# Grouped attention: own buffer for the query squares, result copies ahead of the upper halves, first lower half ahead of the next inverse sum

## The chip, the core and the metric

The kernel runs on one core of a Trainium2 chip. The metric is the time of one execution in microseconds (us) on the device; a shorter time is better. A core has five engines that run their own instruction streams and wait for each other through semaphores: TensorE (PE, matrix products, with PEld for its weight loads), VectorE (DVE), ScalarE (ACT), GpSimd (POOL) and SyncE (SP), which issues most DMAs.

## What is computed

The reference is a two layer block. Only the third stage is touched by the change, cross attention with grouped keys. Cut to that stage:

```python
q = (hidden_states @ Wq).reshape(B, S, N_HEADS, HEAD_DIM)            # B 4, S 256, 16 heads of 128
k = (encoder_hidden_states @ Wk).reshape(B, S_enc, N_KV_HEADS, HEAD_DIM)   # 1601 keys, 4 key heads
v = (encoder_hidden_states @ Wv).reshape(B, S_enc, N_KV_HEADS, HEAD_DIM)
q = rms_norm(q, q_norm_w)
k = rms_norm(k, k_norm_w)
scores = jnp.einsum('bqhd,bkhd->bhqk', q, jnp.repeat(k, 4, axis=2)) * scale
probs = jax.nn.softmax(scores, axis=-1)
out = jnp.einsum('bhqk,bkhd->bqhd', probs, jnp.repeat(v, 4, axis=2))
return out.reshape(B, S, N_HEADS * HEAD_DIM) @ Wo
```

Around it stand another attention, a mixture of experts and a quantized feed forward layer.

## The kernel before

`grouped_attention` works in 16 groups (4 batch rows times 4 key heads) of 8 steps, 128 steps in all, numbered n; s = n % 8 is the step within a group g. A step is one query head and one tile of 128 queries against all 1601 keys. A pair of steps (both query tiles of a head) is a unit u. Every value that goes into a product is split into an upper (HI) and a lower (LO) half, and each product is three matmuls.

The order on each engine is written out by hand; nothing is scheduled automatically. In step n:

- PE: `score(n)` fills the four banks of `ps_s`, and may start when ACT's first exponential of step n-1 has read them; then `weigh`, half of the value products of unit n//2 - 2, into `ps_m` (even n starts a unit and waits for `u_here`, odd n ends it); then the jobs of `plan[n]`, which prepare the next group in a ring of three banks `ps_t`: `kv` (keys and values), `q`, `qT` and `kT` (transposes), `y` (output product).
- DVE: `largest(n)` (maximum of the scores, `neg_max`); then its part of `plan[n-1]` (`entry`: copies, lower halves, sums of squares); `invert(n)`, the inverse of the row sum, which waits for both exponentials of step n; `probs_low(n-1)`, the lower halves of the probabilities of the step before in two pieces of 1024 and 577 columns.
- ACT: `exp(n, 0)`, `exp(n, 1)`; `probs_high(n)`, the upper halves, which wait for the inverse sum (`inverted`) and for the transposes of step n-2 (`turned_through`); `take_values` (odd n: `ps_m` to `out_n`, which raises `u_here`) or `split_result` (even n: `out_n` to `oT`, after which POOL subtracts); its part of `plan[n]` (`ring`); splits of weights (`split_q`, `split_kv`, `split_out`, each followed by a subtraction on POOL) in some steps.
- SP: per step one transposing DMA of the lower half of step n-1, then one of the upper half of step n, from `halves` to `pT`; and loads.

ACT's `ring` squares queries and keys into one buffer, `squares_of`, of two key places; a query job fills both. DVE sums them (`tensor_reduce` into `q_sq` or `k_sq`) and raises `squares`. The lines that guard the buffer:

```python
nth = nth_squared[e]
both = kind == "q" or (nth and squared[nth - 1][0] == "q")
if nth - (not both) > 0:
    act.wait_ge(squares, nth - (not both))
```

In a full group, step 0 prepares `qT`, `q`, `kv`; step 1 `q`, `kv` and `q_eps`; steps 2 and 3 two `kv` each (step 2 and 4 also `k_eps`, after which POOL scales); step 4 `kv`, `qT`; step 5 two `kT`; step 6 `y` and two `kT`; step 7 `y`. The last group has no `q`, `kv` or `kT` left to prepare.

Of the kernel before, what the change touches and what calls it, by code (L numbers as in the profile page):

```python
# [14 lines left out]
P = 128  # L15
# [1439 lines left out]
def grouped_attention(nc, side, mix, x_sb, eye, half_power, encoder_t, wq, wk, wv, wo, q_norm_w, k_norm_w):  # L1455
# [110 lines left out]

    squared = [e for n in range(-1, N + DRAIN) for e in plan[n] if e[0] in ("q", "kv")]
    nth_squared = {e: n for n, e in enumerate(squared)}

    with ExitStack() as ctx:  # L1570
        r = Room(nc, ctx, "ga")
# [26 lines left out]
        probs = [sb(f"probs{i}", [P, KV]) for i in range(PB)]  # L1598
        warm = sb("warm", [P, 1])
        squares_of = sb("squares_of", [P, 2, 2, DH])  # L1600
        part_max = sb("part_max", [P, 2])
        neg_max = sb("neg_max", [P, 2])
        half_sum = sb("half_sum", [P, 4, 2])
# [266 lines left out]
        def _(act):  # L1870
# [22 lines left out]
            def ring(e):  # L1893
                kind, m, g = e
                if kind in ("q", "kv"):
                    nth = nth_squared[e]
                    both = kind == "q" or (nth and squared[nth - 1][0] == "q")
                    if nth - (not both) > 0:

                        act.wait_ge(squares, nth - (not both))  # L1900
                act.wait_ge(*filled(e))
                if kind == "q":
                    nc.scalar.activation(squares_of[:, :, :, :].rearrange("p a b d -> p (a b d)"), ps_t[:, bank_of(e), :],
                                         ACT.Square).then_inc(read, 1)
                elif kind == "kv":
                    at, top, src = kv_view(e)
                    nc.scalar.activation(v[g % 3][0:top, HI, at, :], src[:, :, 1, :], ACT.Copy,
                                         scale=side.v_scale[0:top, 0:1])
                    nc.scalar.activation(squares_of[0:top, nth % 2, 0:at.stop - at.start, :], src[:, :, 0, :], ACT.Square
                                         ).then_inc(read, 1)  # L1910
                else:
                    src, dst = ring_parts(e)
                    scale = qk_w[:, 0:1] if kind == "kT" else 1.0
                    nc.scalar.activation(dst(HI), src, ACT.Copy, scale=scale).then_inc(read, 1)
# [41 lines left out]
            for n in range(N + DRAIN):  # L1956
                g, s = n // STEPS, n % STEPS
                if n < N:
                    exp(n, 0)
                    exp(n, 1)  # L1960
                    probs_high(n)
                if n % 2 and 0 <= (n - 5) // 2 < UNITS:
                    take_values((n - 5) // 2)
                if n % 2 == 0 and 0 <= n // 2 - 3 < UNITS:
                    split_result(n // 2 - 3)
                for e in plan[n]:
                    if e[0] == "enc":
                        split_encoder(e[1], e[2])
                    elif e[0] in RING and e[0] != "y":
                        ring(e)  # L1970
                if n == 0:
                    split_q(1)
                if n == 2:
                    split_kv(2)
                if n == 4:
                    split_out(0)
                if s == (5 if g else 6) and g + 2 < GROUPS:
                    split_q(g + 2)
                if s == 2 and 1 < g <= GROUPS:
                    split_out(g - 1)  # L1980
                if s == 7 and 0 < g and g + 2 < GROUPS:
                    split_kv(g + 2)

        @block.vector
        def _(dve):
# [37 lines left out]
            def ring(e):  # L2023
                kind, m, g = e
                if kind == "y":
                    dve.wait_ge(*filled(e))
                    if g:
                        dve.wait_ge(*emptied(("y", m, g - 1)))
                    tile = g // G * QT + m
                    nc.vector.tensor_tensor(x_sb[:, tile, :], x_sb[:, tile, :], ps_t[:, bank_of(e), 0:D], ALU.add  # L2030
                                            ).then_inc(empty, 1)
                    return
                if kind == "q":
                    dve.wait_ge(*copied(e))
                    nc.vector.tensor_copy(qn[:, m, :], ps_t[:, bank_of(e), :]).then_inc(empty, 1)
                    nc.vector.tensor_reduce(q_sq[:, m * HG:(m + 1) * HG],
                                            squares_of[:, :, :, :].rearrange("p a b d -> p (a b) d"), AX.X, ALU.add
                                            ).then_inc(squares, 1)
                    return
                if kind == "kv":  # L2040
                    at, top, src = kv_view(e)
                    dve.wait_ge(*copied(e))
                    nc.vector.tensor_copy(kn[0:top, at, :], src[:, :, 0, :])
                    nc.vector.scalar_tensor_tensor(v[g % 3][0:top, LO, at, :], src[:, :, 1, :], side.v_scale[0:top, 0:1],  # L2044
                                                   v[g % 3][0:top, HI, at, :], ALU.mult, ALU.subtract).then_inc(empty, 1)
                    nc.vector.tensor_reduce(k_sq[0:top, at], squares_of[0:top, nth_squared[e] % 2, 0:at.stop - at.start, :],
                                            AX.X, ALU.add).then_inc(squares, 1)
                    return
                dve.wait_ge(*copied(e))
                if kind == "kT":  # L2050
                    src, dst = ring_parts(e)
                    nc.vector.scalar_tensor_tensor(dst(LO), src, qk_w[:, 0:1], f32(dst(HI)), ALU.mult, ALU.subtract
                                                   ).then_inc(empty, 1)
                else:
                    src, dst = ring_parts(e)
                    nc.vector.tensor_tensor(dst(LO), src, f32(dst(HI)), ALU.subtract).then_inc(empty, 1)
# [27 lines left out]
                dve.wait_ge(summed, n + 1)  # L2084
                nc.vector.reciprocal(inv_sum[:, n % 2:n % 2 + 1], row_sum[:, n % 2:n % 2 + 1]).then_inc(inverted, 1)  # L2085

            def probs_low(n):
                if n >= 2:
                    dve.wait_ge(*turned_through(n - 2))
                for k, (a, z) in enumerate(((0, SPLIT), (SPLIT, KV))):  # L2090
                    dve.wait_ge(high, 2 * n + k + 1)
                    nc.vector.scalar_tensor_tensor(halves[n % 2][:, LO, a:z], probs[n % PB][:, a:z],  # L2092
                                                   inv_sum[:, n % 2:n % 2 + 1], halves[n % 2][:, HI, a:z],
                                                   ALU.mult, ALU.subtract).then_inc(low, 1)

            dve.wait_ge(cleared, 1)
            dve.wait_ge(w_q_hi, 1)
# [4 lines left out]
            for n in range(N + DRAIN + 1):  # L2102
                if n < N:
                    largest(n)
                if n:
                    for e in plan[n - 1]:
                        entry(e)
                if n < N:
                    invert(n)
                if 0 <= n - 1 < N:  # L2110
                    probs_low(n - 1)

        @block.tensor
        def _(pe):
# [497 lines left out]
```

## Time and profile before

| | |
|---|---|
| three runs | 1518.6 us median (1516.31 to 1524.07) |
| the profiled execution | 1521.84 us, span 1519.9 us |
| mean granted TensorE clock | 0.947 of full speed |
| engines' share of the span | PE 82%, DVE 79%, ACT 66%, POOL 35% |
| exponentials of the 128 steps | 469.8 to 1419.9 us, some 950 us |

The profile is one execution. The page gives each engine's busy time; the list of waits says which engine sat idle until which other engine's instruction; the timeline lists instructions by start, merged where alike, with the idle time ahead and its releaser in brackets. A row of the windows gives the stretch, its length, then for PE, PEld, DVE, ACT and POOL the busy time with the number of instructions, then the granted TensorE clock, the busy share of the DMA engines and GB/s. The stretches of the eight steps run from one step's first score product to the next's, steps 0 to 7 of one group.

### The profile page before, as it was taken

The numbers are of one execution on the slowest core, as the hardware profiler recorded it, in microseconds if no ns is written. First come the engines' busy times: TensorE is split into PE (matmuls) and PEld (weight loads), VectorE is DVE, ScalarE is ACT, GpSimd is POOL, SyncE is SP. The second block draws the span as 40 slices with busy tenths as digits, with TensorE's granted clock in tenths as the row PEclk, the third lists the DMA queues.
The fourth block names the chain that finished last, engine by engine and source line by source line (L and its number), as shares of the span: only waits on it lengthen the run. The fifth ranks groups of instructions, "written<-read, shape, count | busy, mean of one in ns | idle before, by whom it ended". The sixth has DMA issues, their size and how long they took to land. (4 is left out here: it accounts for less than half of the span.)

```text
span 1519.9 us, 24089 instructions
## 1 busy us (share of the span) xinstructions
PE 1247.8 (82%) x8420; PEld 1104.7 (73%) x8423; DVE 1193.6 (79%) x2252; ACT 1002.5 (66%) x1834; POOL 534.0 (35%) x419
## 2 busy tenths in 40 slices
PE   5897648888856788989898989998989989988645
PEld 5887637877745677878787878888878888787513
DVE  4676478888857788988878888889888798897377
ACT  4667237787735556777767777677686676776435
POOL 2432243443234442433323334324244143231134
PEclk9999769999978899999999999999999999999878
DMA  6233069899824767778777867687777777768510
GB/s 214 87 129 99 33 225 295 295 294 303 284 69 99 154 138 153 140 142 151 128 134 142 172 135 145 126 152 139 158 147 142 134 131 140 135 122 146 110 56 28
DMA packets 499696, 228.99 MB, mean 151 GB/s; under 512 B 441236, under 2 KB 479256, under 8 KB 499192
## 3 DMA queue, kind: packets, MB, share of 16 engines
q1 hardware_dynamic: 495016, 214.99, 62.5%
q0 software_dynamic: 4560, 12.46, 2.9%
q8 instruction: 68, 1.11, 0.3%
q14 instruction: 52, 0.43, 0.1%
HBM read 106.41 MB, written 11.93 MB: 78 GB/s over the span
## 5 line engine op out<-in xcount | busy, mean ns | idle before, releaser
L2092 DVE SCALAR_TENSOR_TENSOR ga_halves<-ga_probs,ga_inv_sum,ga_halves 128x1024 f16<-128x1024 f32 (+1 forms) x256 | 298.9, 1209 | 0.3 <-issue 0.3
L1924 ACT ACTIVATE ga_probs<-ga_ps_s,ga_neg_max 128x1200 f32<-128x1200 f32 (+1 forms) x256 | 235.5, 928 | 94.6 <-DVE ga_neg_max L2077 90.9
L1932 ACT ACTIVATE ga_halves<-ga_probs,ga_inv_sum 128x1024 f16<-128x1024 f32 (+1 forms) x256 | 233.3, 958 | 93.5 <-DVE ga_inv_sum L2085 63.4
L2117 PE MATMUL ga_ps_m<-ga_pT,ga_v 128*128 128x256 f16 (+1 forms) x1560 | 184.4, 273 | 26.4 <-ACT ga_out_n L1940 26.4
L2072 DVE TENSOR_REDUCE ga_part_max<-ga_ps_s 128x1 f32<-128x1200 f32 x128 | 179.3, 1401 | 26.9 <-PE ga_ps_s L2117 25.5
L2117 PEld LDWEIGHTS ga_ps_m<-ga_pT,ga_v 128*128 128x128 f16 (+1 forms) x1560 | 146.9, 98 | 61.7 <-issue 45.4
L2117 PE MATMUL ga_ps_s<-side_kT,ga_qT 128*128 128x400 f32 (+1 forms) x768 | 159.5, 358 | 19.2 <-ACT ga_probs L1924 15.3
L2117 PE MATMUL ga_ps_t<-side_w_kv,side_encT 128*128 128x256 f32 (+1 forms) x1170 | 157.9, 285 | 18.7 <-DVE ga_v L2044 11.2
L2117 PE MATMUL ga_ps_s<-ga_kT,ga_qT 128*128 128x400 f32 (+1 forms) x768 | 160.2, 359 | 13.0 <-ACT ga_probs L1924 12.0
L2117 PEld LDWEIGHTS ga_ps_t<-side_w_kv,side_encT 128*128 128x128 f32 (+1 forms) x1170 | 145.7, 184 | 25.3 <-DVE ga_v L2044 13.0
L2117 PEld LDWEIGHTS ga_ps_s<-side_kT,ga_qT 128*128 128x128 f32 x768 | 141.2, 195 | 24.8 <-ACT ga_probs L1924 18.3
L2117 PEld LDWEIGHTS ga_ps_s<-ga_kT,ga_qT 128*128 128x128 f32 x768 | 141.7, 196 | 18.0 <-ACT ga_probs L1924 11.5
L2117 PE MATMUL ga_ps_m<-ga_pT,side_v 128*128 128x256 f16 (+1 forms) x936 | 113.3, 278 | 22.1 <-ACT ga_out_n L1940 16.1
L1815 POOL TENSOR_TENSOR ga_oT<-ga_out_n,ga_oT 128x256 fp32r<-128x256 f32 x64 | 54.6, 853 | 215.4 <-ACT ga_oT L1948 215.4
L1287 DVE TENSOR_TENSOR ex_w<-ex_raw,ex_w 128x1408 fp32r<-128x1408 f32 x63 | 105.3, 1671 | 27.2 <-ACT ex_w L1158 25.3
L2117 PEld LDWEIGHTS ga_ps_m<-ga_pT,side_v 128*128 128x128 f16 (+1 forms) x936 | 89.7, 100 | 44.2 <-issue 32.9
L1351 PE MATMUL ex_ps_g<-ex_w,ex_xT 128*128 128x448 f32 x378 | 93.3, 383 | 32.5 <-issue 21.1
L1102 POOL DMA_INDIRECT ex_xg<-all_xn_rows,ex_token_u x63 | 69.9, 1110 | 116.5 <-PE ex_ps_x L1422 95.7
L1351 PEld LDWEIGHTS ex_ps_g<-ex_w,ex_xT 128*128 128x128 f32 x378 | 67.4, 191 | 46.5 <-issue 29.3
L2082 DVE TENSOR_SCALAR ga_row_sum<-ga_half_sum 128x1 f32<-128x1 f32 x128 | 27.1, 212 | 88.7 <-ACT ga_probs L1924 88.4
L1158 ACT ACTIVATE ex_w<-ex_raw 128x1408 fp32r<-128x1408 f32 x63 | 87.5, 1389 | 9.3 <-DMA ex_raw<-in_L_ffn_packed 9.2
L1796 POOL TENSOR_TENSOR ga_q_scale<-ga_q_sq_eps,all_half_power 128x8 f32<-128x8 f32 x16 | 26.5, 1654 | 171.2 <-DVE ga_q_sq_eps L2013 171.2
(294 smaller groups left out, 2530.8 us busy)
## 6 DMA issues: line engine op xcount, KB each, us to landing
ex_raw<-in_L_ffn_packed SPq DMA_DIRECT2D x63, 704.0 KB
side_w_q_raw<-in_L_xattn_Wq SPq DMA_DIRECT2D x16, 512.0 KB
side_w_q_raw<-in_L_xattn_Wo SPq DMA_DIRECT2D x16, 512.0 KB, 4.7
mix_y_rows<-ex_y SPq DMA_DIRECT2D x63, 128.0 KB
side_enc<-in_ctx_turned SPq DMA_DIRECT2D x12, 512.0 KB, 4.9
ca_keys<-in_ctx_turned SPq DMA_DIRECT2D x12, 464.0 KB, 5.8
ca_cache<-in_ctx SPq DMA_DIRECT2D x4, 1024.0 KB, 7.2
ga_pT<-ga_halves SPq DMA_TRANSPOSE x256, 4.0
```

Of the source, the lines that this page charges most:

```text
L1102: nc.gpsimd.indirect_dma_start(xg[j % XGS][:, :], None, xn_rows[:, :], bass.IndirectOffsetOnAxis(ap=token_u[:, j:j + 1], axis=0)).then_inc ...
L1158: nc.scalar.activation(w[j % WS][:, HI, :], raw[j % RAWS][:, :], ACT.Copy).then_inc(w_hi, 1)
L1287: nc.vector.tensor_tensor(w[j % WS][:, LO, :], raw[j % RAWS][:, :], f32(w[j % WS][:, HI, :]), ALU.subtract).then_inc(w_lo, 1)
L1351: mm = nc.tensor.matmul(out, lhs(s), rhs(c), start=first and n == 0, stop=last and n == 2)
L1796: nc.gpsimd.tensor_tensor(q_scale[:, :], q_sq_eps[:, :], half_power[:, 0:QT * HG], ALU.pow).then_inc(q_scaled, 1)
L1815: nc.gpsimd.tensor_tensor(oT[:, h, LO, :], out_n[:, :], f32(oT[:, h, HI, :]), ALU.subtract).then_inc(out_lo, 1)
L1924: nc.scalar.activation(dst, src, ACT.Exp, bias=neg_max[:, n % 2:n % 2 + 1], accum_out=half_sum[:, n % 4, k:k + 1]).then_inc(exped, 1)
L1932: nc.scalar.activation(halves[n % 2][:, HI, a:z], probs[n % PB][:, a:z], ACT.Copy, scale=inv_sum[:, n % 2:n % 2 + 1]).then_inc(high, 1)
L2072: nc.vector.tensor_reduce(part_max[:, 0:1], ps_s[:, 0:NB - 1, 0:WIDE], AX.XY, ALU.max)
L2082: nc.vector.tensor_scalar(row_sum[:, n % 2:n % 2 + 1], half_sum[:, n % 4, 0:1], half_sum[:, n % 4, 1:2], 1.0 / PROBS_TOP, ALU.add, ALU.mul ...
L2092: nc.vector.scalar_tensor_tensor(halves[n % 2][:, LO, a:z], probs[n % PB][:, a:z], inv_sum[:, n % 2:n % 2 + 1], halves[n % 2][:, HI, a:z], ...
L2117: mm = nc.tensor.matmul(out, lhs(a), rhs(c), start=first and n == 0, stop=last and n == 2)
```

## The change

Three edits in `grouped_attention`. First, queries get their own buffer `q_squares`, and a squaring waits only for its own kind: a query for the sum of the query before, a `kv` for the sum of the `kv` job two before. Second, ACT does `take_values` or `split_result` ahead of `probs_high` instead of behind it. Third, DVE does the first piece of `probs_low(n-1)` ahead of `invert(n)` and the second behind it. PE, POOL and SP keep their orders, and no instruction is added or taken away.

```diff
--- before.py
+++ after.py
@@ -1566,6 +1566,8 @@
 
     squared = [e for n in range(-1, N + DRAIN) for e in plan[n] if e[0] in ("q", "kv")]
     nth_squared = {e: n for n, e in enumerate(squared)}
+    of_kind = {kind: [e for e in squared if e[0] == kind] for kind in ("q", "kv")}
+    nth_of_kind = {e: n for some in of_kind.values() for n, e in enumerate(some)}
 
     with ExitStack() as ctx:
         r = Room(nc, ctx, "ga")
@@ -1598,6 +1600,7 @@
         probs = [sb(f"probs{i}", [P, KV]) for i in range(PB)]
         warm = sb("warm", [P, 1])
         squares_of = sb("squares_of", [P, 2, 2, DH])
+        q_squares = sb("q_squares", [P, HG * DH])
         part_max = sb("part_max", [P, 2])
         neg_max = sb("neg_max", [P, 2])
         half_sum = sb("half_sum", [P, 4, 2])
@@ -1893,15 +1896,14 @@
             def ring(e):
                 kind, m, g = e
                 if kind in ("q", "kv"):
-                    nth = nth_squared[e]
-                    both = kind == "q" or (nth and squared[nth - 1][0] == "q")
-                    if nth - (not both) > 0:
-
-                        act.wait_ge(squares, nth - (not both))
+                    nth = nth_of_kind[e]
+                    held = nth - (1 if kind == "q" else 2)
+                    if held >= 0:
+
+                        act.wait_ge(squares, nth_squared[of_kind[kind][held]] + 1)
                 act.wait_ge(*filled(e))
                 if kind == "q":
-                    nc.scalar.activation(squares_of[:, :, :, :].rearrange("p a b d -> p (a b d)"), ps_t[:, bank_of(e), :],
-                                         ACT.Square).then_inc(read, 1)
+                    nc.scalar.activation(q_squares[:, :], ps_t[:, bank_of(e), :], ACT.Square).then_inc(read, 1)
                 elif kind == "kv":
                     at, top, src = kv_view(e)
                     nc.scalar.activation(v[g % 3][0:top, HI, at, :], src[:, :, 1, :], ACT.Copy,
@@ -1958,11 +1960,12 @@
                 if n < N:
                     exp(n, 0)
                     exp(n, 1)
-                    probs_high(n)
                 if n % 2 and 0 <= (n - 5) // 2 < UNITS:
                     take_values((n - 5) // 2)
                 if n % 2 == 0 and 0 <= n // 2 - 3 < UNITS:
                     split_result(n // 2 - 3)
+                if n < N:
+                    probs_high(n)
                 for e in plan[n]:
                     if e[0] == "enc":
                         split_encoder(e[1], e[2])
@@ -2034,7 +2037,7 @@
                     dve.wait_ge(*copied(e))
                     nc.vector.tensor_copy(qn[:, m, :], ps_t[:, bank_of(e), :]).then_inc(empty, 1)
                     nc.vector.tensor_reduce(q_sq[:, m * HG:(m + 1) * HG],
-                                            squares_of[:, :, :, :].rearrange("p a b d -> p (a b) d"), AX.X, ALU.add
+                                            q_squares[:, :].rearrange("p (h d) -> p h d", d=DH), AX.X, ALU.add
                                             ).then_inc(squares, 1)
                     return
                 if kind == "kv":
@@ -2043,7 +2046,7 @@
                     nc.vector.tensor_copy(kn[0:top, at, :], src[:, :, 0, :])
                     nc.vector.scalar_tensor_tensor(v[g % 3][0:top, LO, at, :], src[:, :, 1, :], side.v_scale[0:top, 0:1],
                                                    v[g % 3][0:top, HI, at, :], ALU.mult, ALU.subtract).then_inc(empty, 1)
-                    nc.vector.tensor_reduce(k_sq[0:top, at], squares_of[0:top, nth_squared[e] % 2, 0:at.stop - at.start, :],
+                    nc.vector.tensor_reduce(k_sq[0:top, at], squares_of[0:top, nth_of_kind[e] % 2, 0:at.stop - at.start, :],
                                             AX.X, ALU.add).then_inc(squares, 1)
                     return
                 dve.wait_ge(*copied(e))
@@ -2084,14 +2087,14 @@
                 dve.wait_ge(summed, n + 1)
                 nc.vector.reciprocal(inv_sum[:, n % 2:n % 2 + 1], row_sum[:, n % 2:n % 2 + 1]).then_inc(inverted, 1)
 
-            def probs_low(n):
-                if n >= 2:
+            def probs_low(n, k):
+                if n >= 2 and k == 0:
                     dve.wait_ge(*turned_through(n - 2))
-                for k, (a, z) in enumerate(((0, SPLIT), (SPLIT, KV))):
-                    dve.wait_ge(high, 2 * n + k + 1)
-                    nc.vector.scalar_tensor_tensor(halves[n % 2][:, LO, a:z], probs[n % PB][:, a:z],
-                                                   inv_sum[:, n % 2:n % 2 + 1], halves[n % 2][:, HI, a:z],
-                                                   ALU.mult, ALU.subtract).then_inc(low, 1)
+                a, z = ((0, SPLIT), (SPLIT, KV))[k]
+                dve.wait_ge(high, 2 * n + k + 1)
+                nc.vector.scalar_tensor_tensor(halves[n % 2][:, LO, a:z], probs[n % PB][:, a:z],
+                                               inv_sum[:, n % 2:n % 2 + 1], halves[n % 2][:, HI, a:z],
+                                               ALU.mult, ALU.subtract).then_inc(low, 1)
 
             dve.wait_ge(cleared, 1)
             dve.wait_ge(w_q_hi, 1)
@@ -2105,10 +2108,12 @@
                 if n:
                     for e in plan[n - 1]:
                         entry(e)
+                if 0 <= n - 1 < N:
+                    probs_low(n - 1, 0)
                 if n < N:
                     invert(n)
                 if 0 <= n - 1 < N:
-                    probs_low(n - 1)
+                    probs_low(n - 1, 1)
 
         @block.tensor
         def _(pe):
```

On DVE, step 2 of a full group, from the negated maximum `ga_neg_max` to the next step's first maximum; before:

```order
L2077 TENSOR_REDUCE ga_neg_max<-ga_part_max 128x1
L2035 COPY ga_qn<-ga_ps_t 128x512
L2036 TENSOR_REDUCE ga_q_sq<-ga_squares_of 128x4
L2043 COPY side_kn<-ga_ps_t 128x256
L2044 SCALAR_TENSOR_TENSOR ga_v<-ga_ps_t,side_v_scale,ga_v 128x256
L2046 TENSOR_REDUCE side_k_sq<-ga_squares_of 128x2
L2013 TENSOR_SCALAR ga_q_sq_eps<-ga_q_sq 128x8
L2082 TENSOR_SCALAR ga_row_sum<-ga_half_sum 128x1
L2085 RECIPROCAL ga_inv_sum<-ga_row_sum 128x1
L2092 SCALAR_TENSOR_TENSOR ga_halves<-ga_probs,ga_inv_sum,ga_halves 128x1024
L2092 SCALAR_TENSOR_TENSOR ga_halves<-ga_probs,ga_inv_sum,ga_halves 128x577
```

and after the change (line numbers moved by three):

```order
L2080 TENSOR_REDUCE ga_neg_max<-ga_part_max 128x1
L2038 COPY ga_qn<-ga_ps_t 128x512
L2039 TENSOR_REDUCE ga_q_sq<-ga_q_squares 128x4
L2046 COPY side_kn<-ga_ps_t 128x256
L2047 SCALAR_TENSOR_TENSOR ga_v<-ga_ps_t,side_v_scale,ga_v 128x256
L2049 TENSOR_REDUCE side_k_sq<-ga_squares_of 128x2
L2016 TENSOR_SCALAR ga_q_sq_eps<-ga_q_sq 128x8
L2095 SCALAR_TENSOR_TENSOR ga_halves<-ga_probs,ga_inv_sum,ga_halves 128x1024
L2085 TENSOR_SCALAR ga_row_sum<-ga_half_sum 128x1
L2088 RECIPROCAL ga_inv_sum<-ga_row_sum 128x1
L2095 SCALAR_TENSOR_TENSOR ga_halves<-ga_probs,ga_inv_sum,ga_halves 128x577
```

The 1024 column piece of `ga_halves` moved from behind the reciprocal to ahead of the row sum, and the query sum reads `ga_q_squares`.

On ACT, step 1 of a full group, from the exponentials to the ring's last job; before:

```order
L1924 ACTIVATE ga_probs,ga_half_sum<-ga_ps_s,ga_neg_max 128x1200
L1924 ACTIVATE ga_probs,ga_half_sum<-ga_ps_s,ga_neg_max 128x401
L1932 ACTIVATE ga_halves<-ga_probs,ga_inv_sum 128x1024
L1932 ACTIVATE ga_halves<-ga_probs,ga_inv_sum 128x577
L1940 ACTIVATE ga_out_n<-ga_ps_m,side_out_scale 128x256
L1885 ACTIVATE side_encT<-side_enc 128x2x512
L1903 ACTIVATE ga_squares_of<-ga_ps_t 128x512
L1907 ACTIVATE ga_v<-ga_ps_t,side_v_scale 128x256
L1909 ACTIVATE ga_squares_of<-ga_ps_t 128x256
```

and after:

```order
L1926 ACTIVATE ga_probs,ga_half_sum<-ga_ps_s,ga_neg_max 128x1200
L1926 ACTIVATE ga_probs,ga_half_sum<-ga_ps_s,ga_neg_max 128x401
L1942 ACTIVATE ga_out_n<-ga_ps_m,side_out_scale 128x256
L1934 ACTIVATE ga_halves<-ga_probs,ga_inv_sum 128x1024
L1934 ACTIVATE ga_halves<-ga_probs,ga_inv_sum 128x577
L1888 ACTIVATE side_encT<-side_enc 128x2x512
L1906 ACTIVATE ga_q_squares<-ga_ps_t 128x512
L1909 ACTIVATE ga_v<-ga_ps_t,side_v_scale 128x256
L1911 ACTIVATE ga_squares_of<-ga_ps_t 128x256
```

The copy into `ga_out_n` moved ahead of the two pieces of `ga_halves`, and the query squares go to a buffer of their own.

## Rows read from the trace of the kernel before

**Rows 1.** The page: span, and busy time of each engine.
```profile
span 1519.9 us, 24089 instructions
PE 1247.8 (82%) x8420; PEld 1104.7 (73%) x8423; DVE 1193.6 (79%) x2252; ACT 1002.5 (66%) x1834; POOL 534.0 (35%) x419
```

**Rows 2.** Windows, eight steps: us, busy PE PEld DVE ACT POOL, clock, DMA.
```profile
949.99:958.36 8.37, 7.90 (x58) 7.09 (x56) 6.56 (x12) 6.19 (x11) 1.26 (x1) 1.00 0.79 145
958.36:966.15 7.79, 7.44 (x50) 6.33 (x48) 5.34 (x10) 3.60 (x9) 0.75 (x1) 1.00 0.77 169
966.15:974.62 8.47, 7.61 (x58) 7.07 (x59) 6.68 (x13) 5.54 (x12) 0.27 (x1) 1.00 0.56 108
974.62:983.16 8.54, 7.30 (x56) 6.72 (x55) 8.12 (x15) 6.48 (x14) 4.75 (x3) 1.00 0.49 100
983.16:989.23 6.07, 5.71 (x46) 5.17 (x44) 6.00 (x14) 5.20 (x11) 5.86 (x3) 1.00 0.74 85
989.23:995.23 6.00, 5.52 (x42) 4.68 (x40) 5.83 (x13) 4.61 (x11) 1.49 (x3) 1.00 1.05 234
995.23:1002.97 7.74, 6.64 (x51) 6.10 (x51) 6.62 (x10) 6.64 (x12) 4.14 (x3) 1.00 0.74 141
1002.97:1009.36 6.39, 5.97 (x45) 5.33 (x43) 5.46 (x10) 4.89 (x10) 0.97 (x2) 1.00 0.73 138
```

**Rows 3.** Waits of PE, 560 to 1400 us: us, times, longest.
```profile
PE ga_ps_m L2117 <- ACT ga_out_n L1940: 37.6, 52, 1.8
PE ga_ps_t L2117 <- DVE ga_v L2044: 9.9, 8, 1.3
```

**Rows 4.** Waits of ACT, 560 to 1400 us.
```profile
ACT ga_halves L1932 <- DVE ga_inv_sum L2085: 55.6, 92, 2.3
ACT ga_v L1907 <- DVE ga_q_sq L2036: 47.9, 16, 4.2
ACT side_v L1907 <- DVE ga_q_sq L2036: 30.0, 10, 4.9
ACT ga_halves L1932 <- DMA ga_pT<-ga_halves: 23.0, 20, 2.0
```

**Rows 5.** Waits of DVE, 560 to 1400 us.
```profile
DVE ga_row_sum L2082 <- ACT ga_probs L1924: 68.1, 81, 2.0
```

**Rows 6.** Timeline, step 7 and the next step's first products: start, us, instruction.
```profile
1005.35 1.40 DVE L2072 TENSOR_REDUCE ga_part_max<-ga_ps_s 128x1 f32<-128x1200 f32 x1
...
1007.26 0.16 DVE L2077 TENSOR_REDUCE ga_neg_max<-ga_part_max 128x1 f32<-128x2 f32 x1
...
1007.45 1.26 ACT L1924 ACTIVATE ga_probs<-ga_ps_s,ga_neg_max 128x1200 f32<-128x1200 f32 x1 [1.02 <-DVE ga_neg_max L2077]
...
1009.42 0.21 DVE L2082 TENSOR_SCALAR ga_row_sum<-ga_half_sum 128x1 f32<-128x1 f32 x1 [0.80 <-ACT ga_probs L1924]
...
1009.74 2.02 DVE L2092 SCALAR_TENSOR_TENSOR ga_halves<-ga_probs,ga_inv_sum,ga_halves 128x1024 f16<-128x1024 f32 x2
...
1009.86 1.82 ACT L1932 ACTIVATE ga_halves<-ga_probs,ga_inv_sum 128x1024 f16<-128x1024 f32 x2 [0.48 <-DVE ga_inv_sum L2085]
...
1011.59 0.45 ACT L1940 ACTIVATE ga_out_n<-ga_ps_m,side_out_scale 128x256 f32<-128x256 f32 x1
...
1012.18 2.45 PE L2117 MATMUL ga_ps_m<-ga_pT,ga_v 128*128 128x256 f16 x21 [0.49 <-ACT ga_out_n L1940]
```

**Rows 7.** Timeline, inside the second and the fourth window of rows 2.
```profile
964.11 0.47 ACT L1907 ACTIVATE side_v<-ga_ps_t,side_v_scale 128x256 f16<-128x256 f32 x1 [4.20 <-DVE ga_q_sq L2036]
...
974.11 0.16 DVE L2013 TENSOR_SCALAR ga_q_sq_eps<-ga_q_sq 128x8 f32<-128x8 f32 x1
...
975.19 3.66 DVE L2092 SCALAR_TENSOR_TENSOR ga_halves<-ga_probs,ga_inv_sum,ga_halves 128x1024 f16<-128x1024 f32 x2
...
976.06 2.17 POOL L1800 TENSOR_TENSOR ga_qn<-ga_qn,ga_q_scale 128x1024 f32<-128x1024 f32 x1
```

**Rows 8.** Windows: one step of the last group.
```profile
1381.41:1387.74 6.33, 4.91 (x33) 4.12 (x33) 4.26 (x7) 4.11 (x8) 0.00 (x0) 1.00 0.85 162
```

## The prediction

> **What bounds the kernel now.** I first read the page's engine shares: PE 82%, DVE 79%, ACT 66% [rows 1], so no engine is full, and the stages have to be read apart. The touched stage holds some 950 us. I cut one of its full groups into its eight steps, from one first score product to the next [rows 2]. The steps sum to 59.37 us. In them PE is busy 54.09, DVE 50.61 and ACT 43.15 us, at the full granted clock. PE is thus nearest to full and idle 5.28 us a group; DVE is second, and in steps 4 and 5 it is busy 6.00 of 6.07 and 5.83 of 6.00 us, so there DVE sets the pace.
>
> The lists of waits over 560 to 1400 us (840 us, 14.2 groups) say what PE misses. The largest entry is the value products waiting for ACT's copy `ga_out_n`, 37.6 us in 52 cases [rows 3], 2.6 us a group, half of PE's idle time. Next is a `kv` product waiting for its bank, 9.9 us. On ACT, a copy that waits for DVE's sum of query squares takes 47.9 + 30.0 us in 26 cases [rows 4]; that is a wait of 3 us, twice a group, and one with exponentials queued behind it: in the shown group ACT stands 4.20 us at 964.11 [rows 7]. DVE waits 68.1 us for exponentials ahead of its row sum [rows 5], 4.8 us a group.
>
> The timeline of step 7 shows how the three are chained [rows 6]. Maximum 1005.35 to 1007.42, exponentials from 1007.45, row sum 1009.42 after 0.80 us of waiting, both lower pieces 2.02 us, next maximum 1011.67. That is a loop of 6.32 us. Beside it ACT makes the upper halves for 1.82 us from 1009.86, only then copies `ga_out_n` (0.45 us), and PE's value products start at 1012.18 after waiting 0.49 us.
>
> **The change, part by part.** No instruction is added; what counts is who is in front of whom.
>
> *Result copies first.* `ga_out_n` no longer stands behind the inverse sum and 1.82 us of upper halves. In the timeline the exponentials end near 1009.3, so the copy would end near 1009.8 and not at 1012.04. PE wants it some 2.4 us after the first score product (the next starts at 1009.36, so 1011.7 [rows 2, 6]). The wait of 2.6 us a group goes. The upper halves lose nothing, because ACT then idles 0.48 us for the inverse sum anyway [rows 6], and the copy (0.40 to 0.45) fits in there. Without that cover it would cost 0.45 us a step on ACT, which has 16 us of idle time a group [rows 2].
>
> *Query squares.* ACT's `kv` job of step 0 no longer waits for DVE to sum the query's squares, which DVE does only behind the next maximum. The 4.20 us stand goes, and the exponentials of step 1, queued behind this job, start when `neg_max` is there. The same again in step 2. What is late next is PE itself: step 1 has 7.44 us of PE work in 7.79 [rows 2]. So this gives PE only some 0.3 us directly, and the DVE pair of steps 1 and 2 about 1 us earlier, which lets the maximum of step 2 start with the scores.
>
> *First lower piece ahead of the inverse sum.* The pair takes 2.02 us for 1601 columns [rows 6]; 1024 of them would be 1.3 us by their share, and I take 1.2, as both pieces have a fixed part. In steps where DVE waits for exponentials (0.80 us in step 7) the piece fills the wait. Where DVE has over 2 us of ring jobs, the inverse sum comes 1.2 us later. Behind it on ACT are the upper halves, the ring and the next exponentials; SP's upper transposes are also 1.2 us later, but are needed two steps on. The second lower piece still follows the inverse sum, after 0.8 us instead of 2.0, so SP's lower transpose goes out about 1.1 us sooner after it. This should shrink ACT's 23.0 us of waiting for transposes [rows 4].
>
> **The sum.** Steps 0 to 2: PE work 7.90 + 7.44 + 7.61 = 22.95 us of 24.63 [rows 2]. I leave 0.3 us for a query product that waits for a bank copied behind the maximum: 23.2, a gain of 1.4. Steps 3 to 7: PE work is 7.30 + 5.71 + 5.52 + 6.64 + 5.97 = 31.14 of 34.74 us. DVE is busy 32.03 us in them. That holds a stall of 1.64 us: at 975.19 the pair took 3.66 instead of 2.02 us, while POOL's scaling of the queries ran from 976.06 to 978.23 [rows 7]. In the new order the second piece starts some 1.6 us after the small `q_eps` operation (first piece 1.2, inverse sum 0.3), and POOL's scaling followed that by 1.95 us (974.11 to 976.06 [rows 7]); the stall should go there. Both engines then need about 31 us, and two engines that take turns cannot both be full.
>
> The Trainium skill ("SBUF — State Buffer", Who interferes with whom) has a rule that speaks against the change: a DVE instruction with two SBUF inputs and a GpSimd one that reads SBUF lock each other out for a whole instruction, whichever starts first. The 1.64 us of [rows 7] agree. By the row alone I would count one such stall a group; by the rule, any weight split on POOL that starts ahead of the first piece holds the inverse sum up for its rest.
>
> For these stalls, moved and new, and for exponentials late by ACT's longer queue (from the inverse sum, upper halves of 1.82 us, ring copies and in some steps a weight split, against 0.8 + 2.07 us on DVE to the next `neg_max`) I put 2.3 us on top of 31.1. No row shows this price. Its lower bound is 0, PE's work alone; the upper is 4.5 us, two stalls like the 1.64 and 1.2 us of a late inverse sum once, which eats both gains but for 0.5 us. I take the middle, because POOL is busy only 19.5 of 59.4 us, but 16.2 of them in steps 3 to 6 [rows 2]. So 33.4 us, a gain of 1.3. Per full group 2.7 us; 14 of them: 38 us.
>
> The last group has no `kv` jobs; a step there takes 6.33 us with DVE busy 4.26 and PE 4.91 [rows 8]. The loop loses the 1.2 us piece. The transposes hold it: 0.85 x 6.33 = 5.4 us of DMA a step. So 5.5 us, 0.85 saved in 7 steps: 6 us. The first group waits for gathers; I count nothing there. Sum 44 us.
>
> The profiled execution took 1521.8 us, 1.9 over its span, and 3.2 over the median of the runs. 1521.8 - 44 = 1478; on the scale of the median 1518.6 - 44 = **1475 us**.
>
> **The rivals.**
> 1. *Stalls and a late ACT take most of it back.* Against it: the stalls need POOL at the wrong moment. For it: DVE is full in steps 4 and 5. Price by the upper bound: 0.5 us times 14 plus 6 is 13 us, up to 30: 1489 to 1506. Chance 0.2.
> 2. *All PE idle time goes.* 5.0 us times 14 plus 6 = 76: 1443, and from 1458 on. Against it: DVE would have to be full too. Chance 0.1.
> 3. *No change within 0.5%* (7.6 us, about what can be told). DVE would have to be the bound everywhere, so that PE's waits only move. DVE's 50.6 us a group, with its stall, against 59.4 speak against it. Chance 0.06.
> 4. *Slower: the inverse sum late by the first piece.* Place: steps with over 2 us of ring jobs on DVE, where `invert` comes 1.2 us later and the next exponentials find ACT still in the upper halves and ring. If it passed on in full in six of eight steps, 84 x 1.2 = 101 us, against 5.3 x 14 = 74 us of idle time that can be won: 1546. It decides from 0.9 us a step on. For it: ACT already waits 55.6 us for inverse sums [rows 4]. Against it: scores, maximum and ring leave over 1 us in steps 0 to 2, and ACT idles 16 us a group. Chance 0.04.
>
> **How the numbers follow.** The forecast, 1458 to 1489 around 1475, has 0.6. The range of 1453 to 1504 leaves out the far half of rival 2, the end of rival 1 and rivals 3 and 4 in the main. Faster by over 0.5%: 0.6 + 0.1 and nearly all of rival 1, so 0.87; within: 0.08; slower: 0.05.
>
> **What would show it.** PE's wait for `ga_out_n` near 0; ACT's wait for `ga_q_sq` gone; DVE's wait ahead of the row sum at a third; ACT's wait for inverse sums not much changed, because it moves behind the result copy; step 1 near 7.6, step 3 near 7.3 us; steps 4 to 7 hardly shorter together. Transposes wait less. The prediction is wrong if the lower pieces' mean grows well past its present value, or if the exponentials wait on ACT's own queue and PE's score products wait for them.

## The result, and the profile after

The changed kernel took 1470.38 us (median of 4 runs, 1464.34 to 1472.02) against 1519.82 us beside it, a ratio of 0.9666 with a 95% interval of 0.9628 to 0.9705: 49 us faster, where 44 were forecast (1475 us, range 1453 to 1504).

The page of the changed kernel's profiled execution (1464.34 us) shows:

```profile
span 1462.3 us, 24088 instructions
...
PE 1233.4 (84%) x8420; PEld 1098.3 (75%) x8423; DVE 1206.5 (83%) x2252; ACT 998.6 (68%) x1834; POOL 583.0 (40%) x419
...
L2122 PE MATMUL ga_ps_m<-ga_pT,ga_v 128*128 128x256 f16 (+1 forms) x1560 | 185.1, 274 | 0.0
```

In the page of the kernel before the same row of value products ends in 26.4 us of idle time ahead, all of it for `ga_out_n`:

```profile
L2117 PE MATMUL ga_ps_m<-ga_pT,ga_v 128*128 128x256 f16 (+1 forms) x1560 | 184.4, 273 | 26.4 <-ACT ga_out_n L1940 26.4
```

PE is busy 84% and DVE 83%, against 82% and 79% in [rows 1]. The last column of the value products, idle time ahead, is 0.0 now. Of the 57.6 us between the two profiled spans only some 51 lie in the changed stage: the first score product starts at 459.2 us and not at 465.6, in code that nobody touched, so one pair of profiles can't be compared to better than that. The timed ratio is the measure.

The same group, cut into its steps as in [rows 2] (stretch, length, busy PE, PEld, DVE, ACT, POOL, clock, DMA share, GB/s; the last row sums):

```profile
923.03:930.79 7.76, 7.76 (x57) 7.09 (x56) 6.28 (x12) 6.36 (x12) 2.65 (x2) 1.00 0.84 161
930.79:938.30 7.51, 7.27 (x51) 6.36 (x49) 5.63 (x10) 4.32 (x10) 0.00 (x0) 1.00 1.08 161
938.30:945.64 7.34, 7.34 (x59) 6.93 (x58) 6.92 (x14) 5.17 (x10) 1.02 (x1) 1.00 0.73 143
945.64:952.66 7.02, 7.02 (x56) 6.65 (x55) 6.14 (x15) 6.22 (x12) 4.81 (x4) 1.00 0.62 123
952.66:958.22 5.56, 5.56 (x45) 5.16 (x44) 5.18 (x12) 4.68 (x9) 5.48 (x3) 1.00 0.74 134
958.22:964.70 6.48, 5.53 (x41) 4.68 (x39) 6.30 (x15) 4.75 (x11) 2.87 (x3) 1.00 0.86 192
964.70:971.53 6.83, 6.69 (x51) 6.10 (x51) 6.76 (x11) 6.10 (x11) 3.52 (x3) 1.00 0.74 138
971.53:978.92 7.39, 5.98 (x42) 5.34 (x43) 7.32 (x11) 5.33 (x12) 2.84 (x2) 1.00 0.64 121
sum 55.89, PE 53.16 PEld 48.32 DVE 50.53 ACT 42.92 POOL 23.20; mean PE 6.64 PEld 6.04 DVE 6.32 ACT 5.37 POOL 2.90
```

The group fell from 59.37 to 55.89 us. Steps 0 to 4 are now PE alone (busy 7.76 of 7.76, 7.34 of 7.34, 7.02 of 7.02, 5.56 of 5.56, and 7.27 of 7.51 in step 1). Step 3 gained most, 8.54 to 7.02. PE's own busy time fell as well, from 54.09 to 53.16 us. Steps 5 and 7 got longer (6.00 to 6.48, 6.39 to 7.39), and there DVE is busy 6.30 of 6.48 and 7.32 of 7.39. This is one of the shorter groups: over the 14 groups between the first and the last the mean fell from 60.5 to 57.4 us.

A step of the last group, which took 6.33 us in [rows 8], in the same columns:

```profile
1328.51:1333.96 5.45, 4.76 (x34) 4.09 (x34) 4.71 (x8) 4.11 (x8) 0.00 (x0) 1.00 1.15 207
```

In the timeline of this step the maximum waits for PE's score products, the exponentials for the maximum, and the next score products for the first exponential:

```profile
1328.51 2.45 PE L2122 MATMUL ga_ps_s<-ga_kT,ga_qT 128*128 128x400 f32 x12 [1.26 <-ACT ga_probs L1926]
...
1330.44 1.41 DVE L2075 TENSOR_REDUCE ga_part_max<-ga_ps_s 128x1 f32<-128x1200 f32 x1 [0.24 <-PE ga_ps_s L2122]
...
1332.55 1.26 ACT L1926 ACTIVATE ga_probs<-ga_ps_s,ga_neg_max 128x1200 f32<-128x1200 f32 x1 [0.45 <-DVE ga_neg_max L2080]
...
1333.96 2.46 PE L2122 MATMUL ga_ps_s<-ga_kT,ga_qT 128*128 128x400 f32 x12 [0.69 <-ACT ga_probs L1926]
```

The waits of PE, of ACT and of DVE, over 560 to 1360 us, which is about the same 14 groups:

```profile
PE ga_ps_t L2122 <- DVE all_x L2033: 19.5, 14, 2.4
PE ga_ps_s L2122 <- ACT ga_probs L1926: 10.2, 22, 1.5
```

```profile
ACT ga_halves L1934 <- DVE ga_inv_sum L2088: 134.2, 110, 4.1
ACT ga_probs L1926 <- DVE ga_neg_max L2080: 49.9, 65, 2.8
ACT ga_halves L1934 <- DMA ga_pT<-ga_halves: 3.1, 3, 1.7
```

```profile
DVE ga_part_max L2075 <- PE ga_ps_s L2122: 54.5, 69, 2.8
DVE ga_row_sum L2085 <- ACT ga_probs L1926: 7.0, 16, 0.8
```

Against [rows 3 to 5]: ACT's waits for `ga_q_sq` and PE's for `ga_out_n` are not in the lists any more, DVE's wait ahead of the row sum fell from 68.1 to 7.0 us, and ACT's wait for transposes from 23.0 to 3.1. ACT's wait for inverse sums rose from 55.6 to 134.2 us, and PE has a new longest wait, 19.5 us for the bank of `y` (line `all_x`), 1.4 us in each group.

The timeline of steps 6 and 7 of the group before tells where the new wait comes from:

```profile
914.42 2.40 POOL L1773 TENSOR_TENSOR ga_w_in<-side_w_q_raw,ga_w_in 128x1024 fp32r<-128x1024 f32 x1 [3.23 <-ACT ga_w_in L1876]
...
915.03 2.87 DVE L2095 SCALAR_TENSOR_TENSOR ga_halves<-ga_probs,ga_inv_sum,ga_halves 128x1024 f16<-128x1024 f32 x1
...
916.77 1.72 POOL L1818 TENSOR_TENSOR ga_oT<-ga_out_n,ga_oT 128x256 fp32r<-128x256 f32 x1
917.83 0.20 DVE L2085 TENSOR_SCALAR ga_row_sum<-ga_half_sum 128x1 f32<-128x1 f32 x1
...
921.02 0.42 DVE L2033 TENSOR_TENSOR all_x<-all_x,ga_ps_t 128x256 f32<-128x256 f32 x1
...
921.50 1.69 PE L2122 MATMUL ga_ps_t<-ga_w_out,ga_oT 128*128 128x256 f32 x12 [1.44 <-DVE all_x L2033]
```

POOL starts the subtraction of the next query weights (`split_q`) at 914.42. DVE's first lower piece starts at 915.03 and ends at 917.90, 2.87 us for an operation that takes 1.28 alone. The exponentials ended before 916.2, but the row sum stands behind the piece and starts at 917.83; everything on DVE is late from there, `y` is added only at 921.02, and PE waits 1.44 us for its bank. At 916.77 POOL's next subtraction queues behind DVE in turn, 1.72 us for one of 0.74.

### The profile page after: what moved, and what is told of

It is laid out like the page before. It is cut to its first block and busy times, and to the rows that moved or that the text cites. A ratio compares the mean times of both kernels' runs of the same rounds, so it can differ in the third digit from the quotient of the medians.

```text
span 1462.3 us, 24088 instructions
## 1 busy us (share of the span) xinstructions
PE 1233.4 (84%) x8420; PEld 1098.3 (75%) x8423; DVE 1206.5 (83%) x2252; ACT 998.6 (68%) x1834; POOL 583.0 (40%) x419
## 5 line engine op out<-in xcount | busy, mean ns | idle before, releaser
L2095 DVE SCALAR_TENSOR_TENSOR ga_halves<-ga_probs,ga_inv_sum,ga_halves 128x1024 f16<-128x1024 f32 (+1 forms) x256 | 321.5, 1256 | 0.5 <-issue 0.3
L2122 PE MATMUL ga_ps_t<-side_w_kv,side_encT 128*128 128x256 f32 (+1 forms) x1170 | 154.6, 284 | 2.1 <-POOL ga_halves L1769 1.4
L1818 POOL TENSOR_TENSOR ga_oT<-ga_out_n,ga_oT 128x256 fp32r<-128x256 f32 x64 | 76.2, 1191 | 80.6 <-ACT ga_oT L1950 80.6
L1799 POOL TENSOR_TENSOR ga_q_scale<-ga_q_sq_eps,all_half_power 128x8 f32<-128x8 f32 x16 | 40.0, 2499 | 171.4 <-DVE ga_q_sq_eps L2016 171.4
L1809 POOL TENSOR_TENSOR side_k_scale<-side_k_sq_eps,all_half_power 128x8 f32<-128x8 f32 (+1 forms) x30 | 55.0, 1835 | 82.7 <-DVE side_k_sq_eps L2023 82.6
```

Source lines behind the costliest of these rows:

```text
L1799: nc.gpsimd.tensor_tensor(q_scale[:, :], q_sq_eps[:, :], half_power[:, 0:QT * HG], ALU.pow).then_inc(q_scaled, 1)
L1809: nc.gpsimd.tensor_tensor(k_scale[:, a:z], k_sq_eps[:, a:z], half_power[:, 0:z - a], ALU.pow).then_inc(k_scaled, 1)
L1818: nc.gpsimd.tensor_tensor(oT[:, h, LO, :], out_n[:, :], f32(oT[:, h, HI, :]), ALU.subtract).then_inc(out_lo, 1)
L2122: mm = nc.tensor.matmul(out, lhs(a), rhs(c), start=first and n == 0, stop=last and n == 2)
```

## The experiments

Each kernel was timed beside the kernel before. Together with the change they cover all combinations of its three edits; the others keep GpSimd out of the lower pieces.

**Squares only.**

```diff
-                    if nth - (not both) > 0:
-                        act.wait_ge(squares, nth - (not both))
+                    held = nth - (1 if kind == "q" else 2)
+                    if held >= 0:
+                        act.wait_ge(squares, nth_squared[of_kind[kind][held]] + 1)
```

(with the buffer `q_squares`, and nothing else of the change.)

> Only the query squares get their own buffer and waits; result copies and lower pieces stay as before. My theory (TensorE is the nearest bound, and the whole change won 50 us by taking waits off it): the exponentials of step 1 start 2.4 us sooner, so VectorE is ahead in steps 1 to 3. That takes 0.3 us from step 1, the 0.87 us wait for the result copy from step 2, and the 1.24 us wait of a kv product from step 3: 2.4 us a full group, 34 us in all, 1486 us, range 1480 to 1500. The wait of ScalarE for ga_q_sq is gone, the wait of TensorE for ga_out_n falls from 37.6 to some 25 us. Rival (the squares only move waiting within ScalarE, which idles 16 us a group anyway): under 8 us, 1512 or more.

Measured 1474.47 us, ratio 0.9701 (0.968 to 0.9721): 45 us, 11 more than expected and outside the range of 1480 to 1500, and within noise the whole change. The eight steps of the same group, and their sum:

```profile
924.38:932.75 8.37, 7.90 (x57) 7.09 (x56) 6.56 (x12) 6.18 (x11) 1.26 (x1) 1.00 0.77 145
932.75:940.26 7.51, 7.28 (x51) 6.36 (x49) 5.96 (x13) 4.51 (x11) 0.74 (x1) 1.00 1.05 167
940.26:947.61 7.35, 7.35 (x60) 6.95 (x58) 6.95 (x14) 5.60 (x11) 1.02 (x1) 1.00 0.71 139
947.61:954.63 7.02, 7.02 (x57) 6.64 (x56) 6.15 (x15) 5.89 (x13) 4.15 (x4) 1.00 0.62 127
954.63:960.18 5.55, 5.55 (x45) 5.15 (x44) 5.19 (x10) 4.67 (x10) 5.47 (x3) 1.00 0.72 86
960.18:966.33 6.15, 5.53 (x41) 4.68 (x39) 5.97 (x14) 4.76 (x11) 1.21 (x3) 1.00 1.05 234
966.33:973.96 7.63, 6.65 (x51) 6.11 (x51) 6.63 (x10) 6.53 (x12) 4.14 (x3) 1.00 0.69 130
973.96:980.45 6.49, 5.96 (x45) 5.31 (x44) 5.46 (x10) 4.99 (x11) 0.96 (x2) 1.00 0.74 139
sum 56.07, PE 53.24 PEld 48.30 DVE 48.88 ACT 43.14 POOL 18.96; mean PE 6.66 PEld 6.04 DVE 6.11 ACT 5.39 POOL 2.37
```

Steps 1 to 3 went from 7.79, 8.47 and 8.54 to 7.51, 7.35 and 7.02 us, of which PE is busy nearly all. The three steps won 2.9 us and the others 0.4. PE's wait for `ga_out_n` fell to 20.6 us without being touched. The rival is out.

**Result copies only.**

```diff
                     exp(n, 1)
-                    probs_high(n)
                 if n % 2 and 0 <= (n - 5) // 2 < UNITS:
                     take_values((n - 5) // 2)
                 if n % 2 == 0 and 0 <= n // 2 - 3 < UNITS:
                     split_result(n // 2 - 3)
+                if n < N:
+                    probs_high(n)
```

> Only the result copies go ahead of the upper halves. My theory: the 2.6 us a group of TensorE waiting for ga_out_n go, but steps 1 to 3 keep their late exponentials, so some of it comes back as waits for VectorE's copies: 1.5 to 2.3 us a group, 1487 to 1500 us. The wait for ga_out_n is near 0. Rival (VectorE is the bound and TensorE's waits only change their name): within 8 us of before, 1512 or more.

Measured 1528.4 us, ratio 1.0056 (1.0037 to 1.0076): slower by 9 us, where 1487 to 1500 us were expected. The wait for `ga_out_n` is gone, as forecast, and the gain did not come. In this kernel's timeline of a step 4:

```profile
987.59 0.41 ACT L1948 ACTIVATE ga_oT<-ga_out_n 128x256 fp32r<-128x256 f32 x1
...
988.07 2.57 DVE L2093 SCALAR_TENSOR_TENSOR ga_halves<-ga_probs,ga_inv_sum,ga_halves 128x1024 f16<-128x1024 f32 x2
988.09 0.74 POOL L1815 TENSOR_TENSOR ga_oT<-ga_out_n,ga_oT 128x256 fp32r<-128x256 f32 x1 [0.24 <-ACT ga_oT L1948]
...
990.56 1.39 DVE L2073 TENSOR_REDUCE ga_part_max<-ga_ps_s 128x1 f32<-128x1200 f32 x1
```

The early `split_result` (ACT, 987.59) lets POOL subtract at 988.09 for 0.74 us, just into the lower pieces, which take 2.57 and not 2.02 us [rows 6]. By their recorded starts the piece was even 0.02 us ahead of the subtraction, and it was held all the same. The rival's part, that PE's waits only change their name, is true as well: PE's wait for the bank of `y` grew from 8.4 to 17.9 us.

**Result copies, GpSimd held.** The last kernel with one wait on POOL, ahead of `result_low`:

```diff
+                    if n <= N:
+                        pool.wait_ge(low, 2 * n)
                     result_low(n // 2 - 3)
```

> The kernel before with the second edit alone, and GpSimd's result subtraction held until both lower pieces of the step before are made. e2, the same without the hold, took 1528 us with the lower pieces 0.55 us longer in steps 0, 4 and 6. My theory: those 1.6 us a group are what turned the edit into a loss; without them 1500 to 1512 us. Rival (TensorE's freed time is lost anyway, since VectorE's late copies hold its banks): 1518 or more, step 7 still near 7.9 us.

Measured 1515.29 us, ratio 0.9967 (0.9948 to 0.9986). The hold is worth 13 us, so the collisions made the loss. But the time is 3.3 us beyond the expected range, and step 7 of the shown group is 6.79 against 6.39 us before: even without collisions the edit alone is worth only 0.3%. Both theories hold a part.

**First lower piece only.**

```diff
+                if 0 <= n - 1 < N:
+                    probs_low(n - 1, 0)
                 if n < N:
                     invert(n)
                 if 0 <= n - 1 < N:
-                    probs_low(n - 1)
+                    probs_low(n - 1, 1)
```

> Only the first lower piece goes ahead of the next inverse sum. My theory: VectorE no longer waits 4.8 us a group ahead of the row sum, but the upper halves, and behind them the result copies, come 1.2 us later wherever VectorE has ring work, so the wait for ga_out_n grows from 37.6 to 60 us or more: between 1505 and 1530 us, 1518 most likely. Rival (this edit carries the gain by itself): 1495 or less.

Measured 1512.77 us, ratio 0.996 (0.9938 to 0.9981), within the range. PE's wait for `ga_out_n` grew to 55.3 us, less than the 60 expected, as the upper halves come later. By the two traces the 14 groups between the first and the last took the same as before (846.7 us in both); the gain lies in the last group, 4.7 us, and in the first, 1.8.

**Squares and result copies; squares and first piece; result copies and first piece.** Each is the change without one of its edits.

> Squares and result copies as in the change, the lower pieces both behind the inverse sum as before. My theory: most of the 50 us is here, 35 to 48 us, 1472 to 1485 us, because the third edit only fills VectorE's waits in steps 5 to 7 and pays part of it back at POOL's weight split. Rival (the third edit is what lets the others count, since VectorE is second bound): 1490 or more.

Measured 1481.22 us, ratio 0.9754 (0.9726 to 0.9782). In the range, but slower than the squares alone: the copies cost 7 us here too.

> The changed kernel without its second edit: result copies behind the upper halves as before. Alone that edit cost 8 us on the kernel before and 7 us on top of the squares. If the cost is GpSimd's result subtraction running into the lower pieces, it is there in any order: 1460 to 1466 us. Rival (with the first piece ahead, the inverse sums and upper halves are 1.2 us later, TensorE waits for ga_out_n again as in e3, where it was 55 us, and the second edit earns its place): 1474 or more.

Measured 1498.34 us, ratio 0.9851 (0.9813 to 0.9889): the rival is right, 24 us worse than the squares alone, and the theory of 1460 to 1466 us is out. PE waits again, here over 560 to 1360 us:

```profile
PE ga_ps_m L2121 <- ACT ga_out_n L1942: 50.3, 51, 2.0
```

> Edits two and three without the squares; with it all eight combinations of the three edits are measured. Copies alone cost 9 us, the first piece alone won 7 us, and on top of the squares they turned from minus 7 and minus 24 us singly into plus 4 together. If each of the two makes the other worth having (the piece makes the upper halves late, the early copy makes that harmless), together they win 10 to 30 us here too: 1490 to 1510 us. Rival (they only add up): 1518 to 1524.

Measured 1481.16 us, ratio 0.9758 (0.9722 to 0.9794): the pair wins 39 us, more than expected, where its edits singly gave plus 9 and minus 7.

| squares | copies | first piece | us | ratio |
|---|---|---|---|---|
| yes | | | 1474.47 | 0.9701 |
| | yes | | 1528.4 | 1.0056 |
| | | yes | 1512.77 | 0.996 |
| yes | yes | | 1481.22 | 0.9754 |
| yes | | yes | 1498.34 | 0.9851 |
| | yes | yes | 1481.16 | 0.9758 |
| yes | yes | yes | 1470.38 | 0.9666 |

**The change, GpSimd's `split_q` held** until both lower pieces of its step are made:

```diff
                 if s == (5 if g else 6) and g + 2 < GROUPS:
+                    pool.wait_ge(low, 2 * n + 2)
                     split_q(g + 2)
```

> The changed kernel, and GpSimd's subtraction of the next query weights (split_q) waits until VectorE has made both lower pieces of its step, so that it runs beside VectorE's maximum, which reads PSUM. My theory: in step 6 the first piece is held up 1.62 us by that subtraction, VectorE is late in step 7 and TensorE waits 1.4 us for the bank of y; without it step 7 falls from 7.93 to about 6.6 us: 1.0 to 1.4 us a group, 1450 to 1458 us. Rival (the lateness in step 7 is VectorE's plain load of work): 1465 or more.

Measured 1449.09 us, ratio 0.9531 (0.9484 to 0.9577): 21 us below the change and 1 below the expected range. By the two profiled executions the difference in the stage is 17 us. In its timeline, step 6 and 7:

```profile
963.44 1.28 DVE L2096 SCALAR_TENSOR_TENSOR ga_halves<-ga_probs,ga_inv_sum,ga_halves 128x1024 f16<-128x1024 f32 x1
...
965.84 2.36 POOL L1773 TENSOR_TENSOR ga_w_in<-side_w_q_raw,ga_w_in 128x1024 fp32r<-128x1024 f32 x1 [6.24 <-DVE ga_halves L2096]
965.99 1.41 DVE L2076 TENSOR_REDUCE ga_part_max<-ga_ps_s 128x1 f32<-128x1200 f32 x1 [0.23 <-PE ga_ps_s L2123]
...
968.47 1.70 PE L2123 MATMUL ga_ps_t<-ga_w_out,ga_oT 128*128 128x256 f32 x12
```

The first piece takes 1.28 us again. POOL's subtraction runs from 965.84 beside DVE's maximum, and neither is slower (2.36 and 1.41 us). `y` waits for nothing. The rival is out.

**The change, both held,** that is with the line on `result_low` as well:

> As e5, and GpSimd's result subtraction of every even step waits for both lower pieces of the step before as well. My theory: it also takes the 0.61 us of step 0 and the 0.34 us of step 4 away: 3 to 8 us below e5, 1443 to 1453 us. Rival (those stalls are covered by VectorE's waiting for scores): the same as e5 within 2 us. Second rival (the results come too late for ScalarE's next copy, which waits for them): slower than e5.

Measured 1444.73 us, ratio 0.9512 (0.9467 to 0.9557). Steps 5, 6 and 7 of the same group, and the sum:

```profile
949.43:955.74 6.31, 5.53 (x42) 4.69 (x40) 6.14 (x15) 4.75 (x11) 1.92 (x3) 1.00 0.85 193
955.74:962.57 6.83, 6.70 (x51) 6.11 (x51) 6.76 (x11) 6.10 (x11) 2.30 (x2) 1.00 0.75 142
962.57:968.53 5.96, 5.96 (x43) 5.34 (x43) 5.65 (x11) 5.32 (x12) 3.06 (x2) 1.00 0.71 134
sum 54.30, PE 53.15 PEld 48.33 DVE 48.66 ACT 42.93 POOL 20.61; mean PE 6.64 PEld 6.04 DVE 6.08 ACT 5.37 POOL 2.58
```

Step 7 is 5.96 us, PE alone, as it already was with `split_q` held only, and the group 54.30 us, of which PE is busy 53.15. The 4.4 us against the last kernel lie within both intervals, so the two are not told apart.

**The change, results held, `split_q` not.**

> The changed kernel with GpSimd's result subtraction held until the lower pieces of the step before are made, split_q as in the change. My theory: the 1.62 us of step 6 stays, since split_q causes it, so little is won: 1462 to 1470 us. Rival (the result subtraction is the larger part of what e6 won): 1458 or less.

Measured 1464.73 us, ratio 0.9631 (0.9598 to 0.9664): as expected, little, and not told apart from the change.

**Squares and copies, both held, no first piece.**

> e4 (squares and result copies, both lower pieces behind the inverse sum) with both of e6's holds on GpSimd. It tells what the first piece is worth once GpSimd no longer runs into it: e6 took 1444.7 us. My theory: VectorE waits 4 us a group for the exponentials again, in steps 5 to 0, so this is 15 to 30 us above e6: 1460 to 1475 us. Rival (the holds alone are the gain, the third edit nothing): within 5 us of e6.

Measured 1467.34 us, ratio 0.9658 (0.9623 to 0.9693): in the expected range, and 23 us above the same with the first piece. The third edit earns its place, and earns more once GpSimd is out of its way.

## Why the prediction was right

*The sum.* It was made by stretches of steps, and those held in the shown group: steps 0 to 2 of the group take 22.61 us (forecast 23.2), steps 3 to 7 33.28 (forecast 33.4), and a step of the last group 5.45 (forecast 5.5). The stage's 128 steps went from 949 to 898 us by the two traces, first score product to last: 5.5 us of that in the last group (forecast 6), 2.5 in the first (forecast 0), and 43 in the 14 between, 3.1 a group (forecast 2.7). Two parts of this were luck or wrong in their reason. The sum held PE's work fixed at 54.09 us a group, and it fell by 0.93. And the step of the last group came to 5.45 us, but not because "the transposes hold it": the shown timeline has score products, maximum, first exponential and the next score products waiting for each other, 5.45 us from one first score product to the next. The DMA share, from which 5.4 us had been worked out, went from 0.85 to 1.15 in the shorter step, which by the same product is 6.3 us, so it was no fixed amount of work. ACT waits once for a transpose in 1320 to 1345 us, 0.9 us.

*PE nearest to full, DVE second.* Shown: with the change steps 0 to 4 are PE's work, and with GpSimd held only step 5 keeps more than 0.3 us of PE idle time; DVE is busy 6.14 of its 6.31 us.

*Result copies.* The wait went as forecast, but counting its 2.6 us a group as that edit's gain was wrong. Alone the edit loses 9 us, and with its collisions removed it wins 4. A PE that is let go earlier runs into the next thing that DVE owes it, since DVE's chain of maximum, inverse sum and lower halves did not get shorter. No term of the sum rested on it alone, which is why the total came out.

*Query squares.* "This gives PE only some 0.3 us directly" came out in step 1 (7.79 to 7.51 us). What follows from it had no price of its own, and that was the most mis-sized part: alone the squares are worth 45 us, 3.3 us in the shown group. What I called the DVE pair being 1 us earlier is the gain: it took PE's wait for the copy in step 2 (0.86 us) and for the `kv` bank in step 3 (1.24 us) with it, and also POOL's scaling out of the lower pieces of step 2 (the pair's 1.64 us there are gone in this kernel as well, where both pieces still stand behind the inverse sum).

*First piece.* Right that it fills DVE's wait (68.1 to 7.0 us). ACT's wait for transposes shrank too (23.0 to 3.1), but not by this edit alone: the result copies without it already bring it to 6.8 us. Right too that it makes the inverse sums late; ACT waits 134.2 us for them, which I had said would not change much. That is harmless only because the result copy no longer stands behind: without the second edit the third costs 24 us. So the slower rival named a real mechanism, and the second edit is what disarms it. The 24 us hold both the lateness by the piece itself and that by `split_q` running into it; no run of this pair with `split_q` held tells them apart.

*The stalls.* The 1.64 us of [rows 7] went, as worked out, though the squares alone take them away too. The 2.3 us put on top were for new stalls and lateness, and they were there: steps 3 to 7 take 33.28 us of which PE is busy 30.78, so 2.5. The largest is the one the prediction named, a weight split that starts ahead of the first piece: `split_q` in step 6 is worth 21 us in all by the timed runs, 1.3 in each of 14 groups by the traces. That the middle of the bounds came so near was luck, since no row priced it; the lower bound would have given 1443 us, below the stated range, and the upper 1506, above it.

*The signs.* Steps 4 to 7 together were "hardly shorter", 26.20 and 26.26 us. Of the two signs of being wrong, the lower pieces' mean grew from 1209 to 1256 ns, and PE's wait for exponentials from 3.8 to 10.2 us over 560 to 1360 us: both were there, and small.

*Not additive.* Squares alone win 45, copies with first piece 39, all three 49. On top of the squares the other two take 0.61 us from step 0 and 0.80 from step 6 of the shown group and give back 0.33 in step 5 and 0.90 in step 7, behind the collisions. Over the 14 groups the squares alone and the whole change take the same within noise (801.2 and 803.9 us); what the change has over them lies in the first group (3.2 us) and the last (4.6). That both routes take away the same lateness of DVE, and that this can be won only once, fits these numbers but was argued, not tested by a run. What stays open is how much of the 6.5 us that the profiled spans differ ahead of the stage repeats from run to run.

## What to carry to other kernels

A wait in the list is worth what it costs only if the engine behind it is not late for the next hand-over anyway; removing PE's longest one alone made this kernel slower. Edits that each shorten the same chain of turns are to be judged together, and one that makes a result late may pay only beside another that takes the dependants from behind it. Before an operation is moved on DVE, look at what GpSimd does at the new place, and move that beside an operation with which it did not collide here, the maximum over PSUM.

## What the hardware showed that I had not expected

- How much the collisions cost, and that they cut both ways: a lower piece took 2.87 and not 1.28 us beside a running weight subtraction, a pair 2.57 and not 2.02 us beside one of 0.74 us, and GpSimd's subtraction 1.72 and not 0.74 us behind a piece. The maximum over PSUM (1.40 to 1.41 us) was the same beside GpSimd. This is what the Trainium skill says ("SBUF — State Buffer", Who interferes with whom: a DVE instruction with two SBUF inputs and a GpSimd one that reads SBUF lock each other out, and whichever came first wins). The 2.87 and 1.72 us agree, each with the other engine recorded as first. The 2.57 us do not tell who came first: there the held piece is recorded 0.02 us ahead of GpSimd.
- One wait on GpSimd, which is busy 40% of the span, was worth 21 us of 1470, more than the first piece (7 us) or the result copies (minus 9) give alone.
